# Second attention block: the normalised tokens are turned by VectorE and two transfers through DRAM in place of TensorE transposes, and the way back is one strided transfer everywhere

## The reference

```
def _L1_cond_ref(x, c, w_ada, ...):
    shift_msa, scale_msa, gate_msa, shift_mlp, scale_mlp, gate_mlp = split(silu(c) @ w_ada + b_ada, 6)
    x_mod = (x - mean) * rsqrt(var + EPS) * (1 + scale_msa) + shift_msa
    k, q, v = split(x_mod @ w_qkv, 3)                 # 16 heads of 16 channels
    w = softmax(einsum('bqhc,bkhc->bhqk', q / 16, k))
    y = einsum('bhqk,bkhc->bqhc', w, v)
    x = x + gate_msa * (y @ w_proj + b_proj)
    x = x + gate_mlp * (gelu((_ln(x) * (1 + scale_mlp) + shift_mlp) @ w_mlp1 + b_mlp1) @ w_mlp2 + b_mlp2)
```

## Time and profile before

| | |
|---|---|
| time, median of 3 runs (lowest, highest) | 1572.86 us (1572.06, 1572.91) |
| the profiled execution: time, span | 1573.35 us, 1571.5 us |
| busy share of the span: TensorE matmuls, weight loads | 98%, 88% |
| VectorE, ScalarE, GpSimd | 82%, 56%, 25% |
| DMA: share of its 16 engines on the queue used by SP | 26.5% |
| granted TensorE clock over the span | 0.995 of full |

### The profile page before, as it was taken

How to read it: one execution, slowest core, us unless ns; L and a number is a source line. 1 busy time by engine, 2 the same in 40 slices (tenths; PEclk the granted TensorE clock), 3 DMA queues, 4 the chain that set the end, 5 groups by cost and what they waited for, 6 DMA issues and landing times.

```text
span 1571.5 us, 42382 instructions
## 1 busy us (share of the span) xinstructions
PE 1538.2 (98%) x14314; PEld 1381.8 (88%) x14314; DVE 1294.1 (82%) x2953; ACT 874.9 (56%) x1753; POOL 387.4 (25%) x525
## 2 busy tenths in 40 slices
PE   8999999999999999999999999999997999999999
PEld 7999998999999998677777777777775999999999
DVE  5798888787777787888888888888885888888886
ACT  3566664344444453667777767777765344444443
POOL 2333332010000013243443343443333200000000
PEclk9999999999999999999999999999999999999999
DMA  6700002211111112333333333333331233232232
GB/s 174 223 21 20 20 20 63 77 43 48 47 52 41 53 48 66 109 102 99 109 107 103 108 108 97 107 107 101 107 111 55 83 101 100 94 95 93 100 100 68
DMA packets 147505, 132.84 MB, mean 85 GB/s; under 512 B 23568, under 2 KB 130128, under 8 KB 147424
## 3 DMA queue, kind: packets, MB, share of 16 engines
q1 hardware_dynamic: 147264, 131.74, 26.5%
q0 software_dynamic: 160, 0.04, 0.1%
HBM read 54.75 MB, written 24.54 MB: 50 GB/s over the span
## 4 chain that ended last, share of the span: by engine, by line
PE 91%; DVE 5%; issue 2%; DMA 1%; ACT 1%; DVEq 0%; SPq 0%; POOL 0%; POOLq 0%; ACTq 0%
PE bank L216 63%; PE bank L1788 8%; PE bank L1770 7%; PE bank L1732 5%; PE bank L1798 2%; PE bank L400 2%; PE bank L1806 1%; PE bank L778 1%; PE bank L473 1%; PE bank L198 1%; PE bank L564 0%; DMA A_w_film<-in_L_cond_film_w 0%; DVE C_negmax L1744 0%; DVE m_xhat L1744 0%; DVE m_h_lo L313 0%
## 5 line engine op out<-in xcount | busy, mean ns | idle before, releaser
L1879 ACT ACTIVATE C_probs<-bank 128x1024 f32<-128x1024 f32 x256 | 263.4, 1029 | 156.2 <-PE bank L1770 153.7
L1744 DVE TENSOR_REDUCE C_negmax<-bank 128x4 f32<-128x1024 f32 x248 | 303.4, 1223 | 46.5 <-PE bank L1732 43.0
L1114 ACT ACTIVATE D_g<-bank,D_bias 128x256 f32<-128x256 f32 x256 | 107.5, 472 | 197.7 <-PE bank L216 197.7
L1114 ACT ACTIVATE B_g<-bank,B_bias 128x256 f32<-128x256 f32 x256 | 107.6, 472 | 196.8 <-PE bank L216 196.6
L365 POOL TENSOR_TENSOR m_small<-m_small,consts 128x2 f32<-128x2 f32 x64 | 47.8, 747 | 590.5 <-DVE m_small L359 306.1
L216 PE MATMUL bank<-B_wt_w_hi,B_g_lo 128*128 128x256 f32 x512 | 143.0, 279 | 3.5 <-DVE B_g_lo L1124 3.4
L1770 PEld LDWEIGHTS bank<-C_qs,C_kx 64*128 64x128 f32 x1024 | 77.5, 185 | 78.3 <-ACT C_probs L1879 46.1
L216 PE MATMUL bank<-D_wt_w_hi,D_g_lo 128*128 128x256 f32 x512 | 141.7, 277 | 1.5 <-DVE D_g_lo L1124 1.5
L216 PE MATMUL bank<-m_h_hi,D_wt_w_lo 128*128 128x256 f32 x512 | 141.7, 277 | 0.8 <-DVE m_h_lo L419 0.8
L216 PE MATMUL bank<-m_h_hi,B_wt_w_lo 128*128 128x256 f32 x512 | 141.7, 277 | 0.0
L216 PE MATMUL bank<-B_wt_w_hi,B_g_hi 128*128 128x256 f32 x512 | 141.5, 276 | 0.0
(11 more groups left out here) (267 smaller groups left out, 4835.8 us busy)
## 6 DMA issues: line engine op xcount, KB each, us to landing
C_qs<-C_q_hi SPq DMA_DIRECT2D x128, 128.0 KB
C_kx<-C_k_hi SPq DMA_DIRECT2D x128, 128.0 KB, 2.6
C_qs<-C_q_lo SPq DMA_DIRECT2D x64, 128.0 KB
C_kx<-C_k_lo SPq DMA_DIRECT2D x64, 128.0 KB, 2.1
C_gbc<-mod_rows SPq DMA_DIRECT2D x32, 256.0 KB, 3.4
D_gbc<-mod_rows SPq DMA_DIRECT2D x32, 256.0 KB, 3.4
turned<-N_blocks SPq DMA_DIRECT2D x31, 256.0 KB, 2.0
N_back<-turned SPq DMA_DIRECT2D x124, 64.0 KB, 2.0
```

The source lines that it names most:

```text
L1114: ins = eng.activation(o, p, func, bias=per_seq(bias1, 2 * u + d, b))
L1744: e_max.by(eng.tensor_reduce(m4[:, :, :, j], spair[:, :].rearrange("p (e q k) -> p e q k", e=2, q=TH), AX, ALU.max, negate=True))
L1879: e_exp.by(eng.activation(probs[t % NP][:, :], stpair[:, :], ACT.Exp, scale=scl))
```

## The change

**Phase C.** A `Turn` object is made for C from the third sequence on. The task `T` and its PSUM bank use are gone. VectorE gets `turn` at place 5.9 of its iteration, SP `turn out` at 4.9 and `turn back` at 5. `hi_h` moves in ScalarE's order from 15.465 to 18.7, and `lo_h0` in VectorE's from 8.331 to 9.43. Both now read the fetched tile from SBUF. The tile into which the DMA fetches is the spare buffer `mlp_norm.lo[1]`, the tile that VectorE writes is new (`C_blocks`).

**All phases that turn.** `fetch` is one DMA of 128 partitions with four runs of 512 B each, in place of four DMAs. For that the order of tokens and channels within a block changes: VectorE reads `xhat` with a step of four elements and writes with a step of two, and where the tokens' order is set right again (gelu in B and D, `y_tok` in C), ScalarE reads PSUM with a step of two, and TensorE reads `ysb` with a step of two.

```diff
-                self.e_back = event("turn_back", 16 * QUADS, first)
+                self.e_back = event("turn_back", 16, first)
...
                 n.e_T.by(eng.transpose(
-                    self.blocks.rearrange("p (c t h i) -> p h t c i", c=QUADS, h=TH, t=KT),
-                    n.xhat[:, :].rearrange("p (h t c i) -> p h t c i", c=QUADS, h=TH, t=KT)))
+                    self.blocks.rearrange("p (c t i h) -> p h t c i", c=QUADS, h=TH, t=KT),
+                    n.xhat[:, :].rearrange("p (h t i c) -> p h t c i", c=QUADS, h=TH, t=KT)))
...
             def fetch(self, eng, b):
                 self.e_out.wait(eng, b)
-                for c in range(QUADS):
-                    self.e_back.by(eng.dma_start(
-                        self.back[BLOCK * c:BLOCK * (c + 1), :].rearrange("p (a x) -> p a x", a=QUADS),
-                        turn_dram[:, c * P:(c + 1) * P].rearrange("(a i) x -> i a x", a=QUADS)), 16)
+                self.e_back.by(eng.dma_start(
+                    self.back.rearrange("p (a x) -> p a x", a=QUADS),
+                    turn_dram.rearrange("(a i) (c x) -> (i c) a x", a=QUADS, c=QUADS)), 16)
...
                         if turn.turns(b):
-                            o = o.rearrange("p (h a i) -> p a h i", h=TH, a=QUADS)
-                            p = p.rearrange("p (a h i) -> p a h i", h=TH, a=QUADS)
+                            o = o.rearrange("p (h n) -> p h n", h=TH)
+                            p = p.rearrange("p (n h) -> p h n", h=TH)
...
+                blocks, back = sb("blocks", [P, TH * D]), mlp_norm.lo[1][:, :].bitcast(F32)
...
-                T_PE = {"T": 8.873, "k": 15.427, "q": 23.777, ...
+                T_PE = {"k": 15.427, "q": 23.777, ...
-                T_ACT = {"hi_h": 15.465, ...
+                T_ACT = {"hi_h": 18.7, ...
-                T_DVE = {"stats": 0.622, "lo_h0": 8.331, "lo_h1": 9.442, ...
+                T_DVE = {"stats": 0.622, "turn": 5.9, "lo_h0": 9.43, "lo_h1": 9.442, ...
-                T_SP = {"z0": 13.302, ...
+                T_SP = {"turn out": 4.9, "turn back": 5, "z0": 13.302, ...
...
-                norm = Norm(attention_norm, event, False, scale1a, mbank("T"), (e_v, 1), centred=True)
+                norm = Norm(attention_norm, event, False, scale1a, head_bank, (e_v, 1), centred=True)
+                turn = Turn(norm, event, UNROLL, blocks, back)
...
-                                ins = eng.transpose(mbank("Y1" + "ab"[w])[:, c:c + P],
-                                                    ysb[w][:, g * S + qh * P:g * S + (qh + 1) * P], ident[:, :])
+                                if turn.turns(b):
+                                    tokens = slice(g * S + qh, (g + 1) * S, TH)
+                                else:
+                                    tokens = slice(g * S + qh * P, g * S + (qh + 1) * P)
+                                ins = eng.transpose(mbank("Y1" + "ab"[w])[:, c:c + P], ysb[w][:, tokens], ident[:, :])
```

More of the change, by code:

```diff
@@ L307, in evac_hi, with evac_lo @@
                 n.e_hi.by(ins)
-            def evac_lo(self, eng, b):
+            def evac_lo(self, eng, b, parts=range(KT)):
                 n = self.norm
                 n.e_hi.wait(eng, b)
-                for t in range(KT):
+                for t in parts:
                     ins = eng.scalar_tensor_tensor(out=self.by_block(n.lo[b.par], t), in0=self.tokens(t),
@@ L316, in evac_lo @@
                                                    op0=ALU.mult, op1=ALU.subtract)
-                n.e_lo.by(ins)
+                if KT - 1 in parts:
+                    n.e_lo.by(ins)
         class Norm:
@@ L1559, in phase_l1_attention @@
                         "Y1b": 67.583, "Y2": 68.314, "PR": 75.354}
-                T_ACT = {"hi_h": 15.465, "hi_k": 23.929, "hi_q": 26.206, "vout": 40.131, "exp0": 51.08, "exp1": 51.093,
+                T_ACT = {"hi_h": 18.7, "hi_k": 23.929, "hi_q": 26.206, "vout": 40.131, "exp0": 51.08, "exp1": 51.093,
                          "exp2": 52.512, "exp3": 55.344, "exp4": 56.226, "exp5": 63.134, "exp6": 63.775, "Y0": 65.441,
                          "exp7": 66.356, "Y1": 67.803, "hi_y": 72.581}
-                T_DVE = {"stats": 0.622, "lo_h0": 8.331, "lo_h1": 9.442, "lo_k0": 18.476, "lo_k1": 18.622,
+                T_DVE = {"stats": 0.622, "turn": 5.9, "lo_h0": 9.43, "lo_h1": 9.442, "lo_k0": 18.476, "lo_k1": 18.622,
                          "lo_q0": 22.632, "lo_q1": 23.375, "max0": 26.516, "max1": 31.455, "max2": 34.419,
@@ L1568, in phase_l1_attention @@
                 T_POOL = {"root": 1.041, "xhat": 2.686, "xb": 61.804, "lo_y": 70.105, "res": 76.905}
-                T_SP = {"z0": 13.302, "k0": 18.822, "q0": 23.053, "z1": 25.59, "k1": 25.869, "q1": 32.649, "md0": 36.928,
+                T_SP = {"turn out": 4.9, "turn back": 5, "z0": 13.302, "k0": 18.822, "q0": 23.053, "z1": 25.59, "k1": 25.869, "q1": 32.649, "md0": 36.928,
                         "md1": 45.151, "gates": 57.672}
@@ L1579, in phase_l1_attention @@
                 NEXT_SP = {"D w2": 532, "D turn2": 550, "D gates": 555, "D gates1": 556}
-                BANK = {"T": 1, "q": 2, "k": 1, "v": 2, "Y1a": 2, "Y1b": 0, "Y2": 0, "PR": 0}
+                BANK = {"q": 2, "k": 1, "v": 2, "Y1a": 2, "Y1b": 0, "Y2": 0, "PR": 0}
                 pe_order = schedule(0, T_PE)
@@ L1750, in head_scores @@
                     scores(eng, FIRST, t)
-                NORMED = ("stats", "root", "xhat", "T", "hi_h", "lo_h0", "lo_h1")
+                NORMED = ("stats", "root", "xhat", "turn", "turn out", "turn back", "hi_h", "lo_h0", "lo_h1")
                 TAKEN = [(n, b) for n in NORMED for b in range(2)] + [
@@ L1899, in v_out @@
                         e_vev.by(ins)
-                    tasks = {"hi_h": lambda b: norm.evac_hi(eng, b),
+                    tasks = {"hi_h": lambda b: turn.evac_hi(eng, b),
                              "hi_q": lambda b: hi_bias(eng, b, "q"),
@@ L1982, in gated @@
                             e_tmp.by(ins)
-                    tasks = {"stats": lambda b: norm.stats(eng, b),
+                    tasks = {"stats": lambda b: norm.stats(eng, b), "turn": lambda b: turn.turn(eng, b),
                              "ms0": lambda b: max_split(b, 0), "ms1": lambda b: max_split(b, 1),
@@ L1988, in vector @@
                     for t in range(KT):
-                        tasks[f"lo_h{t}"] = lambda b, t=t: norm.evac_lo(eng, b, parts=(t,))
+                        tasks[f"lo_h{t}"] = lambda b, t=t: turn.evac_lo(eng, b, parts=(t,))
                         tasks[f"lo_q{t}"] = lambda b, t=t: lo_bias(eng, b, "q", parts=(t,))
@@ L2100, in d_gates @@
                         heads["D"].load_gates(eng, seq)
-                    tasks = {"gates": load_gates, "D w2": d_w2, "D turn2": d_turn, "D gates": lambda b: d_gates(b, FIRST),
+                    tasks = {"turn out": lambda b: turn.send(eng, b), "turn back": lambda b: turn.fetch(eng, b),
+                             "gates": load_gates, "D w2": d_w2, "D turn2": d_turn, "D gates": lambda b: d_gates(b, FIRST),
                              "D gates1": lambda b: d_gates(b, SECOND)}
```

7 lines of the change are left out of this document (3 added, 4 removed).

## The result

The changed kernel takes **1637.58 us** (median of 5 runs, 1634.41 to 1638.08) against 1572.91 of the kernel before, run beside it: ratio 1.0401, 95% interval 1.0387 to 1.0414, 64.7 us slower. The prediction named 1616 and a range of 1585 to 1628. The direction was right, and the time lies 9.6 us above the range.

The account below looks back on a forecast made before the run. TensorE was full, but ScalarE's and VectorE's chains stood just behind it, so removing T gained little. 30 iterations x 1.43 = 42.9 us took the profiled 1573.35 to 1616.3, forecast as 1616 us, range 1585 to 1628.

Parts of the forecast that it names:

- The way from mt0 over md0, way back, hi_h and exp0 to ST1: In C's iteration: way back issued 2.44 behind md0, landing 3.0 later, hi_h delays exp0, ST1 comes 1.51 us later.
- simple reading: Rival: TensorE's work is all that counts, so removing T saves 17.7 us, giving 1555 us; chance 0.06.
- B and D were put at 0: In B and D the single fetch and strided accesses cost nothing, since ScalarE and VectorE wait there for TensorE.
- port won: Rival in C: ms0's subtraction starts before POOL's lo_y, way back slow; 1587 to 1599 us, chance 0.16.
- S5's wait (+0.80): In C's iteration: max4 ends at 989.64, so S5 starts then instead of at 988.84, 0.80 us later.
- Its length is 0.71.: VectorE's turn between max3 and ms0 takes 0.71 us, no penalty for the read step; bounded above by twice that.
- the turn is slow: Rival in C: turn takes 1.4 us, ms0's cast is caught too, mt0 0.2 later; 1622 us, inside first case's range.
- the 0.05: In C: ms0's subtraction starts 0.05 us behind POOL's lo_y, so it waits for all of lo_y.
- the main case: In C: VectorE's ms0 loses the port to POOL and way back takes about 3 us; 1616 us, chance 0.50.
- 1.43: Net delay of each C iteration in us: ST1's +1.51 less 0.08 of S0's wait for max7; taken 30 times.
- The ends of C get nothing new: At C's entry and exit the change adds nothing, so no time was priced there.
- The steps of two at Y1a cost nothing by themselves: TensorE's reads of ysb with a step of two add no time, as S5's stepped weight reads take 0.40.

Follow-up runs that it names:

- run 11: Changed kernel, turn an iteration early and without steps, four fetches, ScalarE reordering at ysb, sequences 2 and 3 still transposed by TensorE: 1573.05 us, ratio 0.9994.
- run 3: Changed kernel with POOL's lo_y waiting for mt0 of the same iteration, so nothing of ms0 falls beside it: 1602.04 us, ratio 1.0189.
- run 4: Changed kernel with C's hi_h and lo_h reading C_blocks, not the fetched tile; transfers still issued, output not the reference's: 1634.09 us, ratio 1.0389.
- run 5: Changed kernel with lo_y waiting for mt0 and C's hi_h and lo_h reading C_blocks; output not the reference's: 1590.68 us, ratio 1.0099.
- run 6: Changed kernel with lo_y waiting for mt0, C's hi_h and lo_h reading C_blocks, and turn without steps; output not the reference's: 1579.23 us, ratio 1.0041.
- run 1: Kernel before with only the new block order and single fetch in B and D; C keeps its TensorE transposes: 1573.35 us, ratio 1.0006.
- run 2: Changed kernel with turn reading and writing in the old order, without steps; output not the reference's: 1599.59 us, ratio 1.0183.
- Run 7: Changed kernel with six unused TensorE transposes of ident added between ST6 and S5: 1624.66 us, ratio 1.0322.
- run 10: Changed kernel, turn an iteration early, ScalarE reordering at ysb, single fetch; turn reads with a step of four, writes with none: 1584.45 us, ratio 1.0072.
- the gate: A wait added to the changed kernel: POOL's lo_y waits for mt0 of the same iteration; alone 1602.04 us.
- run 9: Changed kernel, turn an iteration early and without steps, before's block order and four fetches, ScalarE reordering tokens when writing ysb: 1578.19 us, ratio 1.0031.
- run 12: Changed kernel, early turn with stepped read, single fetch, ScalarE reordering at ysb, sequences 2 and 3 still transposed by TensorE: 1579.45 us, ratio 1.0045.
- landing: hi_h's wait for the way back; removed from the changed kernel alone by reading C_blocks in C, 1634.09 us.
- step: The turn's read with a step of four; changed kernel with turn in the old order, without steps, 1599.59 us.

## Why the prediction was right in kind and wrong in size

**What held.** VectorE's row and ScalarE's exponentials, and not TensorE's amount of work, set C: the "simple reading" (1555) is out, since even run 11, without T for 28 sequences and with none of the costs that runs 3 to 6 took away, is level with before. The way from mt0 over md0, way back, hi_h and exp0 to ST1 is, link by link, the one in the trace after, in 19 of the 30 iterations. The way back takes a median of 2.8 from issue to landing (forecast 3.0). The Trainium skill's fit (DMA: Bandwidth & Descriptors, the two cost components) made 2.6. This case's rows have 2.6 for the same fetch in B and 2.8 in C. In the iteration shown it takes 2.95, and hi_h starts 3.18 behind the issue, a little more than the forecast's 3.00. B and D were put at 0 and gave a ratio of 1.0006 whose interval holds 1 (run 1). The rival "port won" (1587 to 1599) is about what run 2 has in its loop, with a turn of 0.70: 0.7 an iteration over before, where the rival had 0.48 to 0.88.

**What failed.** Two steps, one of which was not in the sum at all, and a third that I put at nothing.

*The clock.* I priced S5's wait (+0.80) as time in which TensorE waits, and what it does to the clock at nothing. But behind a wait of 1.05 to 1.15 us the granted clock fell in half of the loop's iterations, and the twelve matmuls of `PR` cost 0.7 to 1.2 us more. Run 7 takes this away and gains 12.9 us (12.4 by the two ratios), with its added work counted in; the loops of the two traces differ by 12.2. Run 7's 1624.7 lies inside the range, so without this term the time would not have left it. It is also in part why run 4 missed. Where the turn is short or the cast isn't caught (runs 2 and 3), the clock does not fall in the loop, so this term came with the next one. Why it falls in one iteration and not in another stays open. The wait's length does not decide it: the first S5 below had waited 1.13 and the clock stayed at 1.00, the second had waited 1.05 and the clock fell (0.57 over the `PR` behind it):

```profile
1028.35 0.51 PE L1734 MATMUL bank<-C_kx,C_qs 64*128 64x256 f32 x4 [1.13 <-DVE C_negmax L1746]
...
1048.21 0.51 PE L1734 MATMUL bank<-C_kx,C_qs 64*128 64x256 f32 x4 [1.05 <-DVE C_negmax L1746]
```

*"Its length is 0.71."* The row that I took the freedom of the step from, a copy of 128 elements, was a small one of another operation, and I read a start of 0.12 into it to make the numbers meet; with the read step of four the turn takes 1.10 (run 10 shows that it is the read). My upper bound of 1.42 held it, and the rival "the turn is slow" named what happened, the cast caught and mt0 later (by 0.2; it was 0.34), for 1622 us. What it does:

- *It changes which instruction loses the port.* At 0.71 the subtraction was to be caught, by 0.05, and in run 2 this is what happens before the loop; in its loop the start moved by some 0.1 and it was not caught, so the 0.05 was too thin to carry the main case. At 1.10 the cast is caught, 0.24 behind lo_y, and mt0 ends 3.83 behind max3's start (1006.95 - 1003.12) instead of the forecast 3.49. ST1 then comes 11.35 behind max3's start, against 9.42 before: 1.93 later, where I had 1.51. Of the 0.42 between them 0.34 are mt0's and 0.18 the way back's up to hi_h; exp0 to ST1 is 0.11 shorter.
- *The Trainium skill's rule* (SBUF — State Buffer, Who interferes with whom), that whoever starts first holds the shared pair of ports for its whole length, agrees with both traces: 1.07 behind lo_y, 0.13 with the gate. The size of this part is a run's: the gate takes away 35.5 us, and the clock's 12.9 are a part of that, since with the gate `PR` is never long.
- *Over all iterations this step is worth less than the 0.42 of one.* In run 7, at full clock, the intervals behind the entry are longer than before's by 1.7 in the loop and 1.2 in the written-out ones, 1.6 in the mean, where I had 1.43.

*The ends.* "The ends of C get nothing new" was wrong by 5 us (4.7 in the first two intervals). In run 9 hi_h of sequence 2 waits at C's entry for a transfer that could not start earlier, and runs 11 and 12, which leave it out, are 5 us shorter. But the wait for the transfer is not all: run 6, where hi_h waits for none, still has 4.0 at the entry, and there TensorE waits 1.88 for the queries' copy, which stands behind the way back on the queue.

So of the 62.6 us by which C is longer, the forecast had 42.9; some 12 are the clock, 4.7 the entry, and the 3 that are left the longer turn and the rest.

**What was small.** "The steps of two at Y1a cost nothing by themselves" is not quite so: the four transposes of `ysb` take 309 ns each with a step (changed kernel, 870:1140) and 287 without (run 9). The first row is the changed kernel's group, the second run 9's:

```profile
L1804 PE MATMUL bank<-ident,C_ysb 128*128 128x128 f32 x108 | 20.2, 309 | 0.0
```

```profile
L1806 PE MATMUL bank<-ident,C_ysb 128*128 128x128 f32 x120 | 19.7, 287 | 0.0
```

That is 0.18 us an iteration on TensorE.

**The parts together.** Gate 35.5, landing 11.4, step 11.4, together 58.3 of 64.7 us. These are prices in this order: taken first, the landing was worth 3.5 and the step 38. Of the 5.7 that are left in run 6, about 4 lie at C's entry by its trace, and about 2 in the iterations behind it.

## What to carry to other kernels

Where an instruction is put among others matters more than what it costs: with the same instructions, 51 of 65 us came back by issuing the turn and its transfers an iteration early, away from the row that a scarce port, a queue and a transfer all hung on. Take a price for a strided access only from the same operation at the same size, and when a length is uncertain, price each of its values by what it makes the neighbours do, not by the difference in length. Before a wait is put into a full TensorE, look at what stands behind it: the matmuls there may run at half clock, as `PR` did in 11 of 22 iterations, and filling the gap with work that nobody needs can be worth more than it costs (12.9 us here).
